# Attention over eight batches: first mixing product over two slots, projections moved, output added by GpSimd, band transposed into the relative products' bank

## The chip, the cores and the metric

The kernel runs on one core of a Trainium2 chip. Five engines work side by side, each through its own list of instructions in order, and meet through semaphores: TensorE (PE; its weight loads are PEld), VectorE (DVE), ScalarE (ACT), GpSimd (POOL) and SyncE (SP), which here only starts DMA transfers. The metric is the device time of one execution in microseconds (us); lower is better.

## What is computed

A block of a network on x of shape 8 x 512 x 128 in float32: attention, mixture of experts, a state-space mixer, the experts again, each behind a layer norm and added to the stream. The change touches attention alone. Cut to what matters:

```python
b, n, _ = x.shape                                  # 8, 512
q, k, v = split(x @ Wqkv.T + bqkv)                 # 16 heads of 64
scores = einsum('bhid,bhjd->bhij', q, k) * SCALE
dist = clip(i - j, -64, 64) + 64
scores = scores + einsum('bhid,ijd->bhij', q, rel_k_emb[dist])
threshold = top_k(scores, 32)[0][..., -1:]         # 32nd largest of each row
attn = softmax(where(scores < threshold, -inf, scores))
v_curr = v
for i in range(3):
    a_v = einsum('bhij,bhjd->bhid', attn, v_curr)
    if i == 0:
        a_v = a_v + einsum('bhij,ijd->bhid', attn, rel_v_emb[dist])
    v_curr = a_v
    res = res + sigmoid(alphas_raw)[i] * v_curr
x = x + merge_heads(res) @ Wout.T + bout
```

## The kernel before

Attention works on one pair of heads of one batch at a time: 8 batches x 8 pairs are 64 iterations (`ITS`). The 512 query rows of an iteration are four tiles T = 0 to 3 of 128 rows, so there are 256 tiles of [128, 2 heads, 512]. All engines run the same order: `run_iterations` calls each engine's `body` once for each *slot*, a pair of iteration i and T, and each body works at that slot on tiles of several ages. `z.back(n)` is the tile that entered n slots ago, `z.iteration(d)` the iteration d away.

For one tile the stages are: at age 0 PE makes the products with the relative keys in banks `RL` and ACT copies them out (`rel`); SP writes them to memory and reads them back skewed (`relj`). At age 2 PE makes the scores in banks `SC`, ACT copies them (`scores`). At age 3 DVE finds the 32 largest of each row: for each head four times `max` (8 values) and three times `match_replace` (L867, L870, L880); POOL then turns the threshold into a mask and adds it (L934 to L949). At age 4 ACT takes exponentials (L794), DVE the reciprocal of the row sums at age 5 (L845, inside `aside`, halfway through the DVE slot) and POOL multiplies (L959). At age 6 PE transposes the probabilities into banks `PT` and ACT copies them to `probs_t`; SP writes a band of them to memory and reads it back skewed (`band`). At age 7 ACT closes the band with sums of what lies left of it, PE transposes it (before: into `PT[0]`) and ACT copies it to `band_t`.

Once an iteration's four tiles are through, three mixing products follow in bank `U`, one of them in each of the slots T = 2, T = 3 and T = 0 of the following iterations. ACT copies each result (`mixed`, L722), PE transposes it, ACT copies it to `u` for the next one, and POOL sums the three with their weights into `res` (L914, L919). At T = 2, three iterations behind, PE multiplies `res` by the output weights in bank `MISC` (L630) and, before the change, DVE adds the result to the stream (L851). The projections to keys (T = 0), values (T = 1) and queries (T = 3) share the bank `MISC` with all this. [...]

`run_iterations` writes iterations -1 to 3 and 62 to 66 out and runs 4 to 61 in a hardware loop of two iterations (8 slots) for each round, on every engine: 29 rounds, 28 jumps back.

Of the kernel before, what the change touches and what calls it, by code (L numbers as in the profile page):

```python
# [16 lines left out]
P = 128  # L17
B, N, D = 8, 512, 128
# [315 lines left out]
class Slots:  # L334


    def __init__(self, g, par, T):
        self.g, self.par, self.i, self.T = g, par, g * 2 + par, T

    def half(self, d):  # L340

        return self.g + (self.par + d) // 2
# [30 lines left out]
def run_iterations(eng, body):  # L373


    first, last = 4, ITS - 2
    for i in range(-1, first):
        for T in range(NT):
            body(Slots(i // 2, i % 2, T), i % 2)
    with eng.Fori(first // 2, last // 2) as g:  # L380
        for par in range(2):
            for T in range(NT):
                body(Slots(g, par, T), par)
    for i in range(last, ITS + 3):
        for T in range(NT):
            body(Slots(i // 2, i % 2, T), i % 2)


def attention(nc, sem, sb, ps, k, t):
# [32 lines left out]
    s.out_made = sem("att_out_made")  # L422
    s.out_added = sem("att_out_added")
    s.bias_added = sem("att_bias_added")
    s.pj_in = [sem(f"att_pj_in{q}") for q in range(2)]
    s.po_in = [sem(f"att_po_in{q}") for q in range(2)]
# [8 lines left out]
    pj = two("pair_j", [P, J_COLS])  # L435
    po = two("pair_o", [P, O_COLS])
    xt = two("xt", [P, N])
# [24 lines left out]

    def mixing(z, par):

        T, old, av = z.T, z.iteration(-3), z.iteration(-2)
        if T == 3 and av is not None:
            return av, 1, par
        if T < 2 and old is not None:
            return old, T + 2, 1 - par
        return None  # L470

    with nc.Block() as block:
        @block.sync
        def _(sp):
            def body(z, par):
                T, q = z.T, z.T % 2
                if T == 2 and (it := z.iteration(1)) is not None:
                    at_pair, at_batch = known(sp, (it % PAIRS) * J_COLS, (it // PAIRS) * N)
                    c0 = known(sp, it - 1)[0]
                    if not early(c0):  # L480
                        sp.wait_ge(s.v_kept, c0)
                    sp.dma_start(pj[1 - par][:, :], t.TJf[:, bass.ds(at_pair, J_COLS)]).then_inc(s.pj_in[1 - par], 16)
                    sp.dma_start(xt[1 - par][:, :], t.XNT[:, bass.ds(at_batch, N)]).then_inc(s.pj_in[1 - par], 16)
                if T == 3 and (it := z.iteration(-1)) is not None:
                    at_out, = known(sp, (it % PAIRS) * O_COLS)
                    c0 = known(sp, it - 1)[0]
                    if not early(c0):
                        sp.wait_ge(s.out_made, c0)
                    sp.dma_start(po[1 - par][:, :], t.TOf[:, bass.ds(at_out, O_COLS)]).then_inc(s.po_in[1 - par], 16)
# [54 lines left out]
        def _(pe):  # L544
# [5 lines left out]
            def body(z, par):  # L550
# [4 lines left out]
                def mix(it, mpar, step):  # L555

                    if not early(it * ORDER + step):
                        pe.wait_ge(s.mixed_kept, it * ORDER + step)
                    for jt in range(NT):
                        for h in range(2):  # L560
                            lhs = v[mpar][:, jt, HEADS[h]] if step == 0 else u[:, jt, h, :]
                            last = nc.tensor.matmul(U[HEADS[h], :], lhs, pt[mpar][:, h, jt, :],  # L562
                                                    start=(jt == 0), stop=(jt == NT - 1 and step > 0))
# [19 lines left out]
                a = z.back(0)  # L583
# [26 lines left out]
                if m and m[1] < 3:  # L610
                    it, step, mpar = m
                    pe.wait_ge(s.mixed_kept, it * ORDER + step)
                    if T == 0 and cur is not None:
                        pe.wait_ge(s.q_kept, cur + 1)
                    if T == 3 and old is not None:
                        pe.wait_ge(s.out_added, old + 1)
                    elif T == 3 and prev is not None:
                        pe.wait_ge(s.v_kept, prev + 1)
                    for jt in range(NT):
# [4 lines left out]
                if T == 2 and old is not None:  # L624
                    pe.wait_ge(s.res_chain, old * 5 + 5)
                    pe.wait_ge(s.po_in[1 - par], 16 * (z.half(-3) + 1))
                    if prev is not None:
                        pe.wait_ge(s.v_kept, prev + 1)
                    for jt in range(NT):
                        last = nc.tensor.matmul(MISC[:, jt * P:(jt + 1) * P], res[:, jt * P:(jt + 1) * P],  # L630
                                                po[1 - par][:, O_W:O_W + P], start=True, stop=True)
                    last.then_inc(s.out_made, 1)

                d = z.back(6)
                if d:
                    it, Td, n = d
                    pe.wait_ge(s.probs, 2 * n + 2)
                    for h in range(2):
                        if h == 0 and not early(n - 1):
                            pe.wait_ge(s.band_kept, n - 1)  # L640
                        elif h == 0 and n > 0:
                            pe.wait_ge(s.probs_kept, 2 * n - 1)
                        if h == 1 and not early(2 * n):
                            pe.wait_ge(s.probs_kept, 2 * n)
# [6 lines left out]
                if T == 0 and cur is not None:  # L651
                    pe.wait_ge(s.pj_in[par], 32 * (z.half(0) + 1))
                    pe.wait_ge(s.q_kept, cur + 1)
                    if m:
                        pe.wait_ge(s.u_kept, m[0] * 2 + 2)
                    nc.tensor.matmul(MISC[:, :], pj[par][:, J_WK:J_WK + P], xt[par][:, :],
                                     start=True, stop=True).then_inc(s.k_made, 1)
                if T == 1 and prev is not None:
# [1272 lines left out]
```

## Time and profile before

| | us |
|---|---|
| median of 3 runs (3132.01 to 3141.05) | 3139.66 |
| the profiled execution, its own time | 3144.04 |
| its span, first to last instruction | 3142.30 |
| attention, from the first `max` of DVE to the end of its last addition to the stream | 64.43 to 2465.46 |

The span is one profiled execution; the profile gives for each engine the busy time, for groups of instructions by line (L867 is line 867) their number, mean duration and what ended the idle time before them, and a timeline. Matmul times are modelled; a releaser is inferred from semaphores, and "issue" stands for time in which an engine waited for nothing that the profile shows. Everything behind 2465 us (experts, mixer, the other norms) is not touched.

### The profile page before, as it was taken

To read this page: it belongs to the slowest core of one execution; us is meant where nothing else is said; L and a number is where in the kernel's file an instruction comes from. 1 tells how busy PE (TensorE), PEld (TensorE's weight loads), DVE (VectorE), ACT (ScalarE), POOL (GpSimd) and SP (SyncE) were. 2 spreads that over 40 slices of the span, in tenths; PEclk is the share of its full clock that TensorE was granted. 3 is DMA by queue.
4 is the path that set the end of the run, shared out by engine and by line. 5 is a ranking of instruction groups with operands and counts; after the bars stand their busy time and mean duration, and the time that the engine had idled before them with its cause. 6 is when DMAs were issued, how large, how long until landed. Compare 5 with 4: busy or idle time off the path is not lost. (4 is left out here: it accounts for less than half of the span.)

```text
span 3142.3 us, 66621 instructions
## 1 busy us (share of the span) xinstructions
PE 2607.6 (83%) x15200; PEld 1498.6 (48%) x15200; DVE 2719.1 (87%) x6639; ACT 2027.7 (65%) x6207; POOL 2163.7 (69%) x2732
## 2 busy tenths in 40 slices
PE   4788888888788888888888888888888685988857
PEld 2444444444444444444444444444444444777743
DVE  5999999999999999999999999999998374765646
ACT  2677777877777777777777777777787152222214
POOL 1788888888888888888888888888888142221105
PEclk7899999999999999999999999999999696776659
DMA  4444444444444444444444444444443000000001
GB/s 119 118 132 134 129 127 125 129 132 125 131 126 129 127 127 127 128 126 130 131 129 126 130 125 134 125 125 131 127 131 100 4 29 14 8 6 1 0 8 48
DMA packets 401017, 318.44 MB, mean 101 GB/s; under 512 B 33246, under 2 KB 388648, under 8 KB 400808
## 3 DMA queue, kind: packets, MB, share of 16 engines
q1 hardware_dynamic: 398660, 314.18, 34.7%
q10 hardware_dynamic: 2148, 2.33, 0.3%
q14 instruction: 182, 1.49, 0.2%
q8 instruction: 27, 0.44, 0.1%
HBM read 139.48 MB, written 136.58 MB: 88 GB/s over the span
## 5 line engine op out<-in xcount | busy, mean ns | idle before, releaser
L870 DVE MAX8 top<-work 128x8 f32<-128x512 f32 x1536 | 980.7, 681 | 0.0
L880 DVE MATCH_REPLACE8 work<-top,work 128x512 f32<-128x512 f32 x1024 | 685.5, 678 | 0.0
L949 POOL TENSOR_TENSOR scores<-scores,cut 128x512 f32<-128x512 f32 x512 | 643.7, 1279 | 0.0
L562 PE MATMUL bank<-probs_t,u 128*64 128x512 f32 x2048 | 467.7, 598 | 1.4 <-ACT u L760 1.4
L794 ACT ACTIVATE probs_of_tile<-scores,minus_max_and_least 128x512 f32<-128x512 f32 x512 | 373.9, 748 | 89.7 <-POOL scores L949 89.2
L959 POOL TENSOR_SCALAR probs_of_tile<-probs_of_tile,inverse 128x512 f32<-128x512 f32 x512 | 349.0, 692 | 84.1 <-DVE inverse L845 61.4
L867 DVE MAX8 top<-scores 128x8 f32<-128x512 f32 x512 | 325.9, 679 | 82.8 <-issue 63.5
L940 POOL TENSOR_SCALAR cut<-scores,minus_max_and_least 128x512 f32<-128x512 f32 x512 | 354.2, 692 | 62.7 <-issue 39.5
L880 DVE MATCH_REPLACE8 work<-top,scores 128x512 f32<-128x512 f32 x512 | 342.7, 678 | 0.0
L771 ACT ACTIVATE probs_t<-bank 128x512 f32<-128x512 f32 x512 | 283.6, 609 | 66.7 <-PE bank L646 66.5
L945 POOL TENSOR_SCALAR cut<-cut 128x512 f32<-128x512 f32 x512 | 305.8, 613 | 21.5
L646 PE MATMUL bank<-identity,probs_of_tile 128*128 128x128 f32 x2048 | 310.9, 302 | 8.5 <-POOL probs_of_tile L959 8.5
L753 ACT ACTIVATE scores<-bank 128x512 f32<-128x512 f32 x512 | 273.5, 584 | 40.6 <-PE bank L605 40.6
L630 PE MATMUL bank<-pair_o,res 128*128 128x128 f32 x512 | 109.5, 382 | 228.7 <-POOL res L919 228.0
L646 PEld LDWEIGHTS bank<-identity,probs_of_tile 128*128 128x128 f32 x2048 | 268.0, 158 | 28.6 <-issue 19.1
L562 PE MATMUL bank<-probs_t,v 128*64 128x512 f32 x1024 | 257.3, 648 | 0.0
L562 PEld LDWEIGHTS bank<-probs_t,u 128*64 128x64 f32 x2048 | 135.7, 136 | 242.2 <-issue 240.4
L934 POOL TENSOR_SCALAR minus_max_and_least<-top 128x4 f32<-128x4 f32 x256 | 50.1, 196 | 238.5 <-issue 194.1
L630 PEld LDWEIGHTS bank<-pair_o,res 128*128 128x128 f32 x512 | 94.3, 276 | 249.4 <-issue 232.3
L731 ACT ACTIVATE band<-band 128x129 f32<-128x129 f32 x512 | 154.3, 303 | 61.6 <-DMA band<-probs_scratch 61.0
L577 PE MATMUL bank<-keys_left,qt 64*128 64x64 f32 (+3 forms) x1024 | 186.1, 441 | 1.8 <-ACT scores L753 1.5
L1634 POOL TENSOR_TENSOR mixer_a_spread<-rest_after,mixer_a 128x1024 f32<-128x1024 f32 x32 | 66.8, 2090 | 174.5 <-PE bank L1491 143.2
(251 smaller groups left out, 5062.7 us busy)
## 6 DMA issues: line engine op xcount, KB each, us to landing
probs_scratch<-probs_of_tile SPq DMA_DIRECT2D x256, 256.0 KB, 2.5
band<-probs_scratch SPq DMA_DIRECT2D x256, 256.0 KB, 3.2
rel_scratch<-rel SPq DMA_DIRECT2D x256, 254.0 KB, 3.1
relj<-rel_scratch SPq DMA_DIRECT2D x256, 128.0 KB, 2.3
relj<-rel_scratch SPq DMA_DIRECT2D x512, 64.0 KB, 2.5
xt<-stream_normed_t SPq DMA_DIRECT2D x64, 256.0 KB, 2.4
pair_j<-table_j SPq DMA_DIRECT2D x64, 193.5 KB, 2.2
pair_o<-table_o SPq DMA_DIRECT2D x64, 66.0 KB, 1.9
```

The costliest lines, as they stand in the source:

```text
L562: last = nc.tensor.matmul(U[HEADS[h], :], lhs, pt[mpar][:, h, jt, :], start=(jt == 0), stop=(jt == NT - 1 and step > 0))
L646: last = nc.tensor.transpose(PT[h][:, jt * P:(jt + 1) * P], t.prob[Td][:, h, HALF + jt * P:HALF + (jt + 1) * P], k.ident[:, :])
L753: nc.scalar.activation(sc[Tb][:, h, :], SC[h][:, :], ACT.Copy).then_inc(s.scores_kept, 1)
L771: nc.scalar.activation(pt[dpar][:, h, :, Td * P:(Td + 1) * P], PT[h][:, :].rearrange("p (j i) -> p j i", j=NT), ACT.Copy).then_inc(s.probs ...
L794: nc.scalar.activation(t.prob[Tx][:, h, HALF:HALF + N], sc[Tx][:, h, :], ACT.Exp, bias=neg[q][:, h, 0:1], accum_out=rs[Tx][:, h:h + 1]).th ...
L867: nc.vector.max(top[q][:, h, 0:8], sc[Tc][:, h, :]).then_inc(s.tops, 1)
L870: nc.vector.max(top[q][:, h, 8 * r:8 * r + 8], work[:, h, :]).then_inc(s.next_tops, 1)
L880: nc.vector.match_replace(out=work[:, h, :], in_to_replace=top[q][:, h, 8 * r:8 * r + 8], in_values=sc[Tc][:, h, :] if r == 0 else work[:, ...
L940: nc.gpsimd.tensor_scalar(cut[:, h, :], sc[Tc][:, h, :], neg[q][:, h, 1:2], STEEP, ALU.add, ALU.mult).then_inc(s.compared, 1)
L945: nc.gpsimd.tensor_scalar(cut[:, h, :], cut[:, h, :], 0.0, NEG, ALU.min, ALU.max).then_inc(s.cut, 1)
L949: nc.gpsimd.tensor_tensor(sc[Tc][:, h, :], sc[Tc][:, h, :], cut[:, h, :], ALU.add).then_inc(s.masked, 1)
L959: nc.gpsimd.tensor_scalar(row, row, inv[Ty][:, h:h + 1], 1.0, ALU.mult, ALU.mult).then_inc(s.probs, 1)
```

## The change

- `run_iterations` has no loop any more: iteration -1, eight batches of eight iterations, and three more iterations are written out. All indices are numbers, so `MISC` products read the tables `table_j`, `table_o` and the normed input where they lie, and the copies to `pair_j`, `xt` and `pair_o` go.
- The first mixing product was made at T = 2, 8 products of 512 columns and 2 for the band. Now columns 0 to 383 are made at T = 1 (with the band for 0 to 255), the rest at T = 2.
- Keys are projected at T = 1, queries at T = 2, both for the next iteration; values at T = 2 after the mixing. ACT copies values at the beginning of T = 3.
- The output product is copied by ACT to `outs` (new), and POOL adds it to the stream; DVE's addition goes.
- The band is transposed into columns 256 to 511 of `RL[0]`, before the probabilities' transposes and not behind them; the next relative product waits until that is copied, and ACT copies it ahead of the exponentials.

```diff
 def run_iterations(eng, body):
-    first, last = 4, ITS - 2
-    for i in range(-1, first):
-        for T in range(NT):
-            body(Slots(i // 2, i % 2, T), i % 2)
-    with eng.Fori(first // 2, last // 2) as g:
-        for par in range(2):
-            for T in range(NT):
-                body(Slots(g, par, T), par)
-    for i in range(last, ITS + 3):
-        for T in range(NT):
-            body(Slots(i // 2, i % 2, T), i % 2)
+    for T in range(NT):
+        body(Slots(-1, PAIRS - 1, T), 1)
+    def batch(g, count=PAIRS):
+        for c in range(count):
+            for T in range(NT):
+                body(Slots(g, c, T), c % 2)
+    for g in range(B):
+        batch(g)
+    batch(B, 3)
...
 # SyncE
-                    sp.dma_start(pj[1 - par][:, :], t.TJf[:, bass.ds(at_pair, J_COLS)]).then_inc(s.pj_in[1 - par], 16)
-                    sp.dma_start(xt[1 - par][:, :], t.XNT[:, bass.ds(at_batch, N)]).then_inc(s.pj_in[1 - par], 16)
...
-                    sp.dma_start(po[1 - par][:, :], t.TOf[:, bass.ds(at_out, O_COLS)]).then_inc(s.po_in[1 - par], 16)
...
 # TensorE
-                a = z.back(0)
+                a, e = z.back(0), z.back(7)
+                if e and not early(e[2]):
+                    pe.wait_ge(s.band_kept, e[2])
...
                 if T == 2 and old is not None:
                     pe.wait_ge(s.res_chain, old * 5 + 5)
-                    pe.wait_ge(s.po_in[1 - par], 16 * (z.half(-3) + 1))
+                    if nxt is not None:
+                        pe.wait_ge(s.k_kept, nxt + 1)
...
+                if e:
+                    pe.wait_ge(s.band_closed, n + 1)
+                    for h in range(2):
+                        last = nc.tensor.transpose(RL[0][:, 2 * P + h * P:2 * P + (h + 1) * P],
+                                                   band[q][:, h, P:2 * P], k.ident[:, :])
+                    last.then_inc(s.band_turned, 1)
...
+                if T == 1 and av is not None:
+                    pe.wait_ge(s.probs_kept, (av * NT + 3) * 2)
+                    pe.wait_ge(s.v_kept, av + 1)
+                    mix(av, par, 0, 0, 3 * P)
+                    pe.wait_ge(s.band_kept, av * NT + 2)
+                    mix_band(0, 2 * P)
+                if T == 2 and av is not None:
+                    pe.wait_ge(s.probs_kept, (av + 1) * NT * 2)
+                    mix(av, par, 0, 3 * P, N)
+                    pe.wait_ge(s.band_kept, (av + 1) * NT)
+                    mix_band(2 * P, N).then_inc(s.mixed, 1)
+                if T == 2 and prev is not None:
+                    if nxt is not None:
+                        pe.wait_ge(s.q_kept, nxt + 1)
...
 # ScalarE
+                if T == 2 and old is not None:
+                    act.wait_ge(s.out_made, old + 1)
...
+                    nc.scalar.activation(outs[:, :], MISC[:, :], ACT.Copy).then_inc(s.out_kept, 1)
...
 # VectorE
-                    if old is not None and T == 2:
-                        dve.wait_ge(s.out_made, old + 1)
...
-                        Xb = k.X[:, bass.ds((old // PAIRS) * N, N)]
-                        nc.vector.tensor_tensor(Xb, MISC[:, :], Xb, ALU.add).then_inc(s.out_added, 1)
...
 # GpSimd
+                if z.T == 2 and (old := z.iteration(-3)) is not None:
+                    pool.wait_ge(s.out_kept, old + 1)
...
+                    Xb = k.X[:, tokens(old)]
+                    nc.gpsimd.tensor_tensor(Xb, outs[:, :], Xb, ALU.add).then_inc(s.out_added, 1)
```

The end of DVE's loop body before, over the jump back (L380), with the last tile of a round; register instructions (L369, L844) stand between the operations:

```order
L867 MAX top<-scores 128x8
L880 MATCH_REPLACE work<-top,scores 128x512 x2
...
L870 MAX top<-work 128x8
L369 REGISTER_ALU
L870 MAX top<-work 128x8
L380 REGISTER_ALU
L380 COMPARE_AND_BRANCH
```

A tile of DVE now; the next one follows it in the list:

```order
L866 MAX top<-scores 128x8 x2
L879 MATCH_REPLACE work<-top,scores 128x512 x2
L869 MAX top<-work 128x8 x2
L879 MATCH_REPLACE work<-top,work 128x512 x2
L850 RECIPROCAL inverse<-row_sums 128x2
L869 MAX top<-work 128x8 x2
L879 MATCH_REPLACE work<-top,work 128x512 x2
L869 MAX top<-work 128x8 x2
```

The jump, the register instructions and the addition L851 are no longer in DVE's list.

PE's slot T = 2 in the loop before (`bank` is any bank; `probs_t,v` is the first mixing product):

```order
L605 MATMUL bank<-relj,identity 64x192 x4
L625 ISA
L626 REGISTER_ALU
L630 MATMUL bank<-pair_o,res 128x128 x4
...
L646 MATMUL bank<-identity,probs_of_tile 128x128 x8
L678 REGISTER_ALU
L680 ISA
L684 MATMUL bank<-identity,band 128x128 x2
...
L562 MATMUL bank<-probs_t,v 64x512 x8
L693 MATMUL bank<-band_t,rel_values 64x512 x2
```

The end of slot T = 1 and slot T = 2 now:

```order
L665 MATMUL bank<-stream_normed_t,table_j 128x512
L554 MATMUL bank<-probs_t,v 64x384 x8
L561 MATMUL bank<-band_t,rel_values 64x256 x2
...
L632 MATMUL bank<-table_o,res 128x128 x4
L641 MATMUL bank<-identity,band 128x128 x2
L653 MATMUL bank<-identity,probs_of_tile 128x128 x8
L673 MATMUL bank<-stream_normed_t,table_j 128x512
L554 MATMUL bank<-probs_t,v 64x128 x8
L561 MATMUL bank<-band_t,rel_values 64x256 x2
L693 MATMUL bank<-table_j,stream_normed_t 128x128 x4
```

Three quarters of the mixing stand in T = 1, the two projections for queries and values in T = 2, and the band ahead of the probabilities.

## Rows read from the trace of the kernel before

**Rows 1.** Windows: straight code, loop, straight code; busy (count) of PE, PEld, DVE, ACT, POOL, clock
```profile
100.00:178.00 78.00, 63.44 (x368) 32.84 (x369) 78.00 (x189) 58.35 (x183) 64.55 (x87) 0.87 0.43 123
178.00:2325.00 2147.00, 1859.75 (x11633) 995.73 (x11629) 2075.07 (x4938) 1650.37 (x5176) 1797.65 (x2383) 0.94 0.45 128
2325.00:2420.00 95.00, 77.85 (x494) 42.79 (x492) 95.00 (x228) 72.75 (x226) 83.84 (x110) 0.95 0.40 114
```

**Rows 2.** The view of line L867, DVE's first max of a tile: idle before (us, times)
```profile
  issue: 63.5, 25
```

**Rows 3.** Timeline of DVE in the loop: start, us, engine, line, operation
```profile
1046.50 1.26 DVE L867 MAX8 top<-scores 128x8 f32<-128x512 f32 x2
...
1051.58 0.67 DVE L851 TENSOR_TENSOR stream<-bank,stream 128x512 f32 x1
...
1055.87 1.27 DVE L867 MAX8 top<-scores 128x8 f32<-128x512 f32 x2
...
1067.52 1.29 DVE L867 MAX8 top<-scores 128x8 f32<-128x512 f32 x2 [2.79 <-ACT scores L753]
```

**Rows 4.** Timeline of DVE, the last tiles, in straight code
```profile
2385.31 1.27 DVE L867 MAX8 top<-scores 128x8 f32<-128x512 f32 x2
...
2411.62 1.27 DVE L867 MAX8 top<-scores 128x8 f32<-128x512 f32 x2
```

**Rows 5.** Timeline of POOL, the first instruction for each tile, slots T = 3 to T = 2
```profile
1029.19 0.20 POOL L934 TENSOR_SCALAR minus_max_and_least<-top 128x4 f32<-128x4 f32 x1 [1.06 <-issue]
...
1046.02 1.27 POOL L919 TENSOR_TENSOR res<-res,tmp 128x512 f32<-128x512 f32 x1
1047.26 0.19 POOL L934 TENSOR_SCALAR minus_max_and_least<-top 128x4 f32<-128x4 f32 x1
...
1056.10 0.20 POOL L934 TENSOR_SCALAR minus_max_and_least<-top 128x4 f32<-128x4 f32 x1 [1.79 <-issue]
```

**Rows 6.** Timeline of PE, one iteration between two jumps
```profile
1020.04 0.60 PE L577 MATMUL bank<-keys_left,qt 64*128 64x192 f32 x4
...
1047.53 1.13 PE L630 MATMUL bank<-pair_o,res 128*128 128x128 f32 x8 [3.15 <-POOL res L919]
1048.49 1.04 PE L646 MATMUL bank<-identity,probs_of_tile 128*128 128x128 f32 x8
1050.30 0.44 PE L684 MATMUL bank<-identity,band 128*128 128x128 f32 x2 [0.77 <-ACT probs_t L771]
1050.66 3.65 PE L562 MATMUL bank<-probs_t,v 128*64 128x512 f32 x16
...
1055.11 0.59 PE L577 MATMUL bank<-keys_left,qt 64*128 64x192 f32 x4
```

**Rows 7.** Timeline of ACT, slots T = 1 and T = 2
```profile
1042.15 0.67 ACT L782 ACTIVATE rel<-bank 128x254 f32<-128x254 f32 x2
...
1046.68 0.31 ACT L731 ACTIVATE band<-band 128x129 f32<-128x129 f32 x1 [1.27 <-DMA band<-probs_scratch]
...
1048.70 1.06 ACT L753 ACTIVATE scores<-bank 128x512 f32<-128x512 f32 x2
...
1050.61 0.67 ACT L782 ACTIVATE rel<-bank 128x254 f32<-128x254 f32 x2
```

**Rows 8.** The view of the tile `band` in the loop: waits for its DMA, time to landing
```profile
  DMA band<-probs_scratch: 54.2, 48
...
DMA to landing us min/median/max: 2.8/3.2/4.0
```

**Rows 9.** Timeline of PE and DVE at attention's start and in its straight code
```profile
51.41 2.08 PE L671 MATMUL bank<-xt,pair_j 128*128 128x512 f32 x2 [4.02 <-DMA xt<-stream_normed_t]
...
64.43 1.29 DVE L867 MAX8 top<-scores 128x8 f32<-128x512 f32 x2 [10.90 <-ACT scores L753]
...
107.33 1.22 PE L592 MATMUL bank<-rel_keys,qt 64*128 64x254 f32 x4 [3.44 <-issue]
```

**Rows 10.** Timeline of DVE at attention's end
```profile
2464.77 0.69 DVE L851 TENSOR_TENSOR stream<-bank,stream 128x512 f32<-128x512 f32 x1 [23.80 <-PE bank L630]
```

More of the change, by code:

```diff
@@ L433, in two @@
         return [sb(f"{name}{q}", shape) for q in range(2)]
-    pj = two("pair_j", [P, J_COLS])
-    po = two("pair_o", [P, O_COLS])
-    xt = two("xt", [P, N])
+    outs = sb("outs", [P, N])
     qt = two("qt", [P, N])
@@ L553, in body, with mix @@
                 cur, nxt = z.iteration(0), z.iteration(1)
-                def mix(it, mpar, step):
-                    if not early(it * ORDER + step):
+                def mix(it, mpar, step, lo=0, hi=N):
+                    if lo == 0 and not early(it * ORDER + step):
                         pe.wait_ge(s.mixed_kept, it * ORDER + step)
@@ L638, in body @@
                     for h in range(2):
[L639 to L644, printed above, removed]
+                        if not early(2 * n + h - 1):
+                            pe.wait_ge(s.probs_kept, 2 * n + h - 1)
                         for jt in range(NT):
@@ new lines, in body @@
+                if T == 2 and nxt is not None:
+                    if old is not None:
+                        pe.wait_ge(s.out_kept, old + 1)
+                    else:
+                        pe.wait_ge(s.k_kept, nxt + 1)
+                    nc.tensor.matmul(MISC[:, :], t.TJ[:, z.pair(1), J_WQ:J_WQ + P], k.XNT[:, tokens(nxt)],
+                                     start=True, stop=True).then_inc(s.q_made, 1)
+                if T == 1 and av is not None:
+                    pe.wait_ge(s.probs_kept, (av * NT + 3) * 2)
+                    pe.wait_ge(s.v_kept, av + 1)
+                    mix(av, par, 0, 0, 3 * P)
+                    pe.wait_ge(s.band_kept, av * NT + 2)
+                    mix_band(0, 2 * P)
@@ L674, in body @@
-                e = z.back(7)
-                if e:
-                    it, Te, n = e
-                    q = Te % 2
-                    pe.wait_ge(s.band_closed, n + 1)
-                    if d:
-                        pe.wait_ge(s.probs_kept, 2 * (n + 1) + 1)
-                    elif not early(n):
-                        pe.wait_ge(s.band_kept, n)
-                    for h in range(2):
-                        last = nc.tensor.transpose(PT[0][:, h * P:(h + 1) * P], band[q][:, h, P:2 * P], k.ident[:, :])
-                    last.then_inc(s.band_turned, 1)
@@ L687, in body @@
-                if T == 2 and av is not None:
-                    pe.wait_ge(s.probs_kept, (av + 1) * 2 * NT)
-                    pe.wait_ge(s.v_kept, av + 1)
-                    mix(av, par, 0)
-                    pe.wait_ge(s.band_kept, (av + 1) * NT)
-                    for h in range(2):
-                        last = nc.tensor.matmul(U[HEADS[h], :], t.relv[:, :], bt[par][:, h, :],
-                                                start=False, stop=True)
-                    last.then_inc(s.mixed, 1)
```

155 lines of the change are left out of this document (74 added, 81 removed).

## The prediction

> **What bounds the kernel now.** I read the windows first [rows 1]. In attention DVE is busy 2075 of the loop's 2147 us and for the whole of the two stretches of straight code around it; PE has 87%, POOL 84%, ACT 77%. So inside attention DVE sets the time, if nobody makes it wait. It does stop: the view of its first `max` of a tile has 25 waits with no releaser, 63.5 us, 2.54 each [rows 2]. The timeline shows what they are [rows 3]. Tile starts at 1046.50 and 1055.87 lie 9.37 apart, with the addition to the stream (L851) between; the next at 1067.52 is 11.65 later, with 2.79 of idle. In the straight code behind the loop three tiles take 26.31, that is 8.77 each [rows 4]. So a tile costs DVE 8.77 us, an addition 9.37 - 8.77 = 0.60 more, and the slot over the loop's jump back some 2.7 more. This row puts the 2.79 down to ACT's score copy, but such gaps come once in eight tiles, 28 times, and 25 of them have no releaser; and ACT's copies of the scores end well ahead, at 1049.76 for the tile that DVE begins at 1055.87, 6.1 later [rows 3, 7]. The gaps are the jump's. Since DVE's list is its own, these three terms must add up: from the first `max` at 64.43 to that of the last tile at 2411.62 are 2347.19 us for 255 tiles [rows 4, 9]. 255 x 8.77 = 2236.4. One addition an iteration falls into 61 of these slots, 61 x 0.60 = 36.6. The rest, 74.2 us, over 28 jumps is 2.65 each, which agrees with the 2.54.
>
> **What goes from the bound.** (1) The jumps: 28 x 2.65 = 74.2 us. The changed DVE list has one tile behind the other, as in the straight stretches of before, where DVE is busy for 78.00 of 78.00 and 95.00 of 95.00 us [rows 1]. The Trainium skill, page "Runtime: NRT & Kernel Launch", section "Instruction fetch mechanics", says that a taken branch to a target outside the two buffered blocks waits for a fetch, while straight code is fetched ahead with the cost mostly hidden; by that rule, too, the gaps go and none comes in their place, and the trace agrees where it has straight code. (2) The additions: 61 inside, and one more for the last tile, 62 x 0.60 = 37.2. Together 111.4 us, 3.5%.
>
> **What the others pay, and whether it stays covered.** After the change DVE asks for an iteration each 4 x 8.77 = 35.08 us; before it was 2347.19 / 63.75 = 36.8. Every other engine must do one in less.
>
> POOL: in an iteration without a jump, 4 x 8.77 + 0.60 = 35.68 long, it stands idle before two of four tiles, 1.06 and 1.79 [rows 5], and works through between the others. Its work is 35.68 - 2.85 = 32.8, the short gaps between instructions among it. The new addition is a two-input operation on 128 x 512, as L919: 1.27 [rows 5]. Makes 34.1, 1.0 under DVE's. It stands where POOL waited 1.79, behind T = 1's tile, so it is hidden: 0 us. POOL is the closest to becoming the bound by its own work. The Trainium skill, "GPSIMD Engine Reference", section "Engine selection", advises against this step: elementwise additions belong on VectorE, GpSimd being about twice as slow for two inputs. The rows agree on the price (1.27 against 0.67), but it is paid on the engine with room. By its factor the change would lose 0.6 us an iteration if both engines were equally full; they are not.
>
> PE: from 1020.04 to 1055.11 an iteration, of which it waited 3.15 and 0.77 [rows 6], so about 31.1 of work at the higher clock. New is only that the mixing is cut in two. A quarter of 3.65 is 0.91; if the 16 passes of 128 columns cost no less than the transposes' passes (1.04 for 8) they take 2.08, so the cut costs 0 to 1.2 us. Work 31 to 32.3 of 35.08. The four slots become even, about 8 each, where T = 1 was short and T = 2 long. PE's added waits: behind `band_closed` stand now the probabilities' transposes; at T = 2 the values wait for the query copy, which ACT makes behind the exponentials. I follow that one, as PE's next scores queue behind it. The exponentials wait for POOL's mask, which follows DVE by some 6 us; copy 0.7, value product 1.0, then 2.1 to the next scores, 1.1 for ACT's copy after the band sums: some 12.5 us behind the end of a DVE tile, and DVE needs them two tiles, 17.5, behind it. 5 us of room; 0 us.
>
> ACT: busy 77%, 28.4 us an iteration; the copy `outs` adds 0.6. Fine by sum, but there is a ring: ACT's `rel` copy ends, SP issues the store and then the load of the band, that lands, ACT makes the band sums, scores, probabilities and `rel` again. In T = 1 to 2 it took from 1042.82 to 1051.28, 8.46, with ACT waiting on the DMA in between [rows 7]. The copy `outs` stands inside it: 8.46 + 0.47 (spacing of the other copies of this size) = 8.93, over 8.77. But only for one slot in four; the others have no `outs`, and in the loop ACT waited on this DMA in 48 of 233 slots [rows 8]. I take a whole iteration at 8.93 + 3 x 8.46 = 34.3 and 0 us, with an upper end of 4 x 8.93 = 35.7, which would be 0.6 x 64 = 40 us.
>
> Transfers: 192 copies of SP (`pair_j`, `xt`, `pair_o`) go from its queue. They were hidden and go at 0 us; the queue they leave also carries the band, so their going speaks for the ring, if anything. At the start PE waited 4.02 for `xt` [rows 9]; without it keys come first (2.1 and ACT's two copies), so queries start at about 52.0 where they started at 51.41: +0.6. At the end, behind DVE's last tile, nothing hides: 23.80 of the last wait is the chain of three mixings for the last iteration [rows 10]. Three quarters of the first one now start before the band is closed, -2.5; the last output goes through ACT (0.6 and a semaphore) and POOL (1.27) and not DVE (0.69), +1.3. Sum -1.2. Between -4 and +3 for both ends together.
>
> **The sum**, against the profiled execution's own 3144.04 (span 3142.30 and 1.74 around it): - 74.2 - 37.2 + 0.6 - 1.2 = 3032. The median of the runs lies 4.4 below that execution, so as a median **3028**.
>
> **Rivals.** (A) DVE stays the bound in every slot: 3028, with 3018 to 3040 for the ends, the clock and the untouched rest. (B) A ring or an engine becomes the bound, at 35.3 to 36.0 an iteration: the ACT and DMA ring at 4 x 8.93, or POOL at 34.1 with its start delayed. For it: a slot at 8.93 and POOL at 97%. Against: both sums are under 35.08, and short delays are taken up by 5 us of room. Price 0.2 to 0.9 x 64 = 13 to 58 us: 3041 to 3086. (C) The jumps' 2.65 are not the jump but the fetch of so many instructions, and the written out list pays it again once in eight to ten tiles: only the additions go, 3028 + 74 = 3102. For it: the gap follows a count of instructions as well as a jump. Against: no gap in 173 us of straight code [rows 1], some 20 tiles. (D) Slower. PE has about ten times DVE's instructions, and its straight code shows one stall of 3.44 us with no releaser, at 107.33 [rows 9]. If written out code brings two such stalls an iteration, PE needs 31.1 + 6.9 = 38.0 against 36.8 before: 3140 + 1.2 x 64 = 3217. It decides from (36.8 - 31.1) / 2 = 2.85 us a stall. Against: one is in the trace, in some ten iterations of straight code, not two in each.
>
> **Chances.** A 0.72, B 0.16, C 0.05, D 0.04, and 0.03 for something between A and less. What a measurement of this kernel can tell from no change is about 0.3%, 9 us; A, B and C are all faster by more. Faster 0.94, same 0.02, slower 0.04. The range takes in A whole and B's lower two thirds: 3014 to 3068.
>
> **What would show it.** Right: tile starts of DVE 8.77 apart throughout, idle before its first `max` 11 us in all, first to last 2236 us; POOL busy about 94% in attention and waiting some 0.5 before T = 2's tile; PE waiting less than 1 before the output product. B: DVE idle before the first `max` with ACT's scores as releaser, spread over many tiles. C: idle marked issue at even distances. D: PE's idle marked issue, growing. Wrong altogether if a tile itself takes DVE longer than 8.77, as when POOL's new addition disturbs it; the rows show it at the same 8.77 whatever POOL does.

## The result

| | before | changed |
|---|---|---|
| median | 3136.55 us (3132.01 to 3141.05, 4 runs) | 3024.56 us (3008.46 to 3027.00, 4 runs) |
| ratio | | 0.963, 95% interval 0.960 to 0.967 |
| the profiled execution, its own time | 3144.04 | 3027.00 |
| its span | 3142.30 | 3025.3 |
| first `max` of DVE's first tile to first `max` of its last tile | 2347.19 | 2235.90 |

The changed kernel is 3.7% faster, 112 us. Of these, 111.3 lie between DVE's first and last tile. The forecast was 3028, and 2236 for that stretch. It started from a median of 3139.66 for the kernel before; the median of all four runs is 3136.55, and this makes up 3.1 of the 3.4 us by which the changed kernel's median lies under the forecast. Below, "the tile stretch" is always this last row: 255 tiles, taken from the starts of the first `max` of each tile in the timeline.

The view of DVE's first `max` of a tile, now L866 (before it had "issue: 63.5, 25" [rows 2]). Columns: line, engine, operation, count; duration in ns, least, median, most; first and last start (the last is the second head's, 0.6 behind the first head's); then what DVE waited for, us and times:

```profile
L866 DVE MAX8 top<-scores x512: 662/665/753, 65.8 to 2302.3; 128x8 f32<-128x512 f32 x171
its engine sat idle before it (us, times) until:
  ACT scores L759: 10.8, 1
```

The one wait is that before the first tile. From there on DVE never stops. The timeline of DVE around 1020 us says the same tile by tile: 8.77 apart, where before the same stretch had 9.37 and 11.65 [rows 3].

```profile
1021.48 1.26 DVE L866 MAX8 top<-scores 128x8 f32<-128x512 f32 x2
...
1030.25 1.26 DVE L866 MAX8 top<-scores 128x8 f32<-128x512 f32 x2
```

The window over nearly all of attention, in the columns of [rows 1]:

```profile
178.00:2285.00 2107.00, 1863.34 (x13208) 1025.75 (x13204) 2107.00 (x5045) 1744.80 (x5404) 1936.59 (x2524) 0.99 0.43 121
```

DVE is busy for 2107.00 of 2107.00 us. POOL is at 1936.59 / 2107 = 92%, PE at 88%, ACT at 83%. PE's granted clock was 0.99 of full speed (2.4 GHz), where it had been 0.94.

PE over slots T = 1 and T = 2 of one iteration, against [rows 6] (start, duration, line, what, idle before and releaser):

```profile
1034.60 2.80 PE L554 MATMUL bank<-probs_t,v 128*64 128x384 f32 x16
...
1039.90 1.16 PE L632 MATMUL bank<-table_o,res 128*128 128x128 f32 x8
1041.08 0.44 PE L641 MATMUL bank<-identity,band 128*128 128x128 f32 x2
...
1043.59 1.09 PE L554 MATMUL bank<-probs_t,v 128*64 128x128 f32 x16
1044.51 0.60 PE L561 MATMUL bank<-band_t,rel_values 128*64 128x256 f32 x4
1046.87 1.16 PE L693 MATMUL bank<-table_j,stream_normed_t 128*128 128x128 f32 x8 [1.76 <-ACT qt L830]
1047.96 0.59 PE L576 MATMUL bank<-keys_left,qt 64*128 64x192 f32 x4
...
1049.45 0.66 PE L606 MATMUL bank<-relj,identity 64*64 64x256 f32 x8
```

The 3.15 us before the output product are gone. In their place PE waits 1.76 before the value product for the query copy. Nothing shows of it on DVE, though the slot is longer than a DVE tile: from one slot's band transposes at 1041.08 to the next slot's at 1050.54 are 9.46 us. POOL in the same iteration, at the places of [rows 5]:

```profile
1021.70 0.20 POOL L940 TENSOR_SCALAR minus_max_and_least<-top 128x4 f32<-128x4 f32 x1 [0.94 <-issue]
...
1046.83 1.27 POOL L925 TENSOR_TENSOR stream<-outs,stream 128x512 f32<-128x512 f32 x1
...
1056.78 0.20 POOL L940 TENSOR_SCALAR minus_max_and_least<-top 128x4 f32<-128x4 f32 x1 [0.97 <-issue]
```

The new addition takes the 1.27 that its neighbour took, and POOL is left with one pause of about 1 us an iteration.

### The profile page after: what moved, and what is told of

It is laid out like the page before. It is cut to its first block and busy times, and to the rows that moved or that the text cites. A ratio compares the mean times of both kernels' runs of the same rounds, so it can differ in the third digit from the quotient of the medians.

```text
span 3025.3 us, 61812 instructions
## 1 busy us (share of the span) xinstructions
PE 2549.6 (84%) x16480; PEld 1500.3 (50%) x16480; DVE 2678.7 (89%) x6575; ACT 2070.2 (68%) x6271; POOL 2245.4 (74%) x2796
## 5 line engine op out<-in xcount | busy, mean ns | idle before, releaser
L866 DVE MAX8 top<-scores 128x8 f32<-128x512 f32 x512 | 327.5, 686 | 10.8 <-ACT scores L759 10.8
L653 PE MATMUL bank<-identity,probs_of_tile 128*128 128x128 f32 x2048 | 276.1, 280 | 6.0 <-POOL probs_of_tile L965 6.0
L554 PE MATMUL bank<-probs_t,v 128*64 128x384 f32 (+1 forms) x2048 | 252.6, 389 | 0.0
L641 PE MATMUL bank<-identity,band 128*128 128x128 f32 x512 | 109.2, 295 | 165.9 <-ACT band L746 164.8
L653 PEld LDWEIGHTS bank<-identity,probs_of_tile 128*128 128x128 f32 x2048 | 240.6, 145 | 6.4 <-POOL probs_of_tile L965 6.4
L554 PEld LDWEIGHTS bank<-probs_t,v 128*64 128x64 f32 x2048 | 124.0, 138 | 171.8 <-ACT probs_t L783 99.1
L796 ACT ACTIVATE rel<-bank 128x254 f32<-128x254 f32 x512 | 174.1, 412 | 2.8 <-PE bank L593 2.8
```

Source lines behind the costliest of these rows:

```text
L554: last = nc.tensor.matmul(U[HEADS[h], lo:hi], lhs, pt[mpar][:, h, jt, lo:hi], start=(jt == 0 and lo == 0), stop=(jt == NT - 1 and step > 0))
L653: last = nc.tensor.transpose(PT[h][:, jt * P:(jt + 1) * P], t.prob[Td][:, h, HALF + jt * P:HALF + (jt + 1) * P], k.ident[:, :])
L866: nc.vector.max(top[q][:, h, 0:8], sc[Tc][:, h, :]).then_inc(s.tops, 1)
```

## The experiments

The forecast had put a price on the jumps and on DVE's addition, and nothing on the three other moves (mixing split, projections moved, band moved). So the first question was whether those moves matter at all, and the later ones followed from the answer. "DVE stretch" is the tile stretch of the profiled execution; the changed kernel's is 2235.90. Each time stands with its ratio to the kernel before from the same chip, since that one moved by a few us between chips (medians 3131.24 to 3139.11).

### 1. The code written out, nothing else (e1_unroll)

```diff
-    with eng.Fori(first // 2, last // 2) as g:
-        for par in range(2):
-            for T in range(NT):
-                body(Slots(g, par, T), par)
+    for i in range(-1, ITS + 3):
+        for T in range(NT):
+            body(Slots(i // 2, i % 2, T), i % 2)
```

> The kernel before with its loop written out and nothing else changed: same order of work, copies of the tables by SyncE, addition to the stream by VectorE. Theory (the 28 gaps belong to the jumps): tile starts 8.77 us apart, 9.37 where an addition lies between, no gap; the time falls by 28 x 2.65 = 74 us, a ratio of 0.976 to the kernel before. Rival (the gaps come with the fetch of so many instructions): no gain, ratio 1.000. Rival (the old order can't keep up without the pauses of the jumps): VectorE waits for ScalarE's scores in many tiles, a ratio between 0.98 and 1.

Measured: 3106.13 us, ratio 0.989 (0.985 to 0.993); DVE stretch 2320.82. Of the 74 us only 26 arrive on DVE and some 30 in the time (29 between the medians, 35 by the ratio), as in the second rival of the expectation. The view of DVE's first `max` shows what came instead of the jumps:

```profile
L859 DVE MAX8 top<-scores x512: 662/676/698, 66.1 to 2387.6; 128x8 f32<-128x512 f32 x171
...
  ACT scores L745: 39.8, 40
```

The jumps' idle is gone, and DVE now waits for ACT's scores, 40 times. The old order can't do an iteration in 35.68 us (four tiles and an addition): it takes 2320.82 / 63.75 = 36.4. The 36.8 of the kernel before hid that.

### 2. Written out, and GpSimd adds the output; the rest in the old order (e2_unroll_pooladd)

On top of experiment 1 ACT's `outs` and POOL's addition of the change, at the same slot.

> As e1_unroll, and the output product copied by ScalarE and added to the stream by GpSimd, still in the old order: first mixing product whole at T = 2, projections at T = 0, 1, 3, band transposed behind the probabilities in their bank. Theory (moving the mixing, the projections and the band takes nothing from VectorE's list and is worth nothing): every tile 8.77 us, ratio 0.964, the same as the full change within 0.2%. Rival (the even order is what lets TensorE and ScalarE keep up at 35.08 us an iteration): VectorE waits for scores, ratio 0.97 or more.

Measured: 3159.60 us, ratio 1.009 (1.006 to 1.011), so 0.9% slower than the kernel before; DVE stretch 2366.55. Both terms of the sum are in this kernel, and both are lost.

```profile
L858 DVE MAX8 top<-scores x512: 666/676/697, 66.1 to 2433.3; 128x8 f32<-128x512 f32 x171
...
  ACT scores L747: 122.4, 80
```

The timelines of one T = 2 slot show the chain, ACT, PE and DVE in turn:

```profile
1022.27 0.31 ACT L725 ACTIVATE band<-band 128x129 f32<-128x129 f32 x1 [1.98 <-DMA band<-probs_scratch]
...
1025.72 1.09 ACT L771 ACTIVATE probs_t<-bank 128x512 f32<-128x512 f32 x2
...
1033.07 0.69 ACT L716 ACTIVATE mixed<-bank,pair_o 128x512 f32<-128x512 f32 x1 [4.03 <-PE bank L687]
...
1035.17 1.09 ACT L747 ACTIVATE scores<-bank 128x512 f32<-128x512 f32 x2 [0.51 <-PE bank L599]
```

```profile
1026.48 0.41 PE L678 MATMUL bank<-identity,band 128*128 128x128 f32 x2 [4.04 <-ACT probs_t L771]
1026.81 5.35 PE L556 MATMUL bank<-probs_t,v 128*64 128x512 f32 x16
...
1032.95 0.59 PE L571 MATMUL bank<-keys_left,qt 64*128 64x192 f32 x4
```

```profile
1035.90 1.29 DVE L858 MAX8 top<-scores 128x8 f32<-128x512 f32 x2 [2.01 <-ACT scores L747]
```

Read it forward. ACT waits for the band's DMA, makes the sums, the scores' copy, `outs` and then the copies of the transposed probabilities. PE waits for the last of these, because the band goes into the same bank. Behind it stands the whole first mixing, and behind that the next tile's score products. PE had stood 4.04 us, and the mixing takes 5.35 instead of the 3.65 of [rows 6]; the window over it shows a granted clock of 0.67 of full speed, the one over the wait before it 1.00 (columns as in [rows 1]):

```profile
1021.00:1026.40 5.40, 1.44 (x14) 1.20 (x12) 5.40 (x14) 4.10 (x15) 2.96 (x4) 1.00 0.64 194
1026.80:1032.00 5.20, 5.20 (x18) 1.61 (x19) 5.20 (x15) 2.24 (x8) 4.87 (x8) 0.67 0.42 117
```

So part of the mixing ran at the lower level, 1.2 GHz. This is not one slot's accident: the page of the profile has 336.6 us for the 64 mixings of this run, 5.26 each, against 257.3 and 4.02 in the kernel before. ACT stands 4.03 us for its result, and the band's next round over DRAM, which ACT has to pass on, starts that much later. Two things in this picture are changed by the change: where the band stands (theory B), and how long the block ahead of the scores is (theory M). Experiments 4 to 7 part them. The lower clock is a third thing, which no run sets by itself: 64 times 5.26 - 3.65 are 103 of the 131 us that this kernel's stretch is longer than the changed kernel's.

### 3. The changed kernel with DVE's addition back (e3_after_dveadd)

DVE adds from the bank, ACT's `outs` and POOL's addition go; the rest is the changed kernel.

> The changed kernel with the addition to the stream back on VectorE, straight from the bank, and no copy by ScalarE. Theory (an addition costs VectorE 0.60 us and nobody else matters): 37 us more than the changed kernel, ratio 0.976 to the kernel before; tiles at 8.77 and one in four at 9.37. Rival (GpSimd's addition costs something back that this kernel regains): less than 30 us more.

Measured: 3063.13 us, ratio 0.976 (0.973 to 0.979); DVE stretch 2274.19, 38.3 more. Two kinds of tile are left, and one in four carries the addition. The timeline of DVE:

```profile
1017.92 1.26 DVE L866 MAX8 top<-scores 128x8 f32<-128x512 f32 x2
...
1023.00 0.66 DVE L850 TENSOR_TENSOR stream<-bank,stream 128x512 f32<-128x512 f32 x1
...
1027.29 1.26 DVE L866 MAX8 top<-scores 128x8 f32<-128x512 f32 x2
```

The first two starts lie 9.37 apart; the next tile, without an addition, begins 8.77 later at 1036.06. The addition's 0.60 was priced rightly (61 x 0.60 = 36.6; two of these tiles took 0.8 and 0.9 longer still).

### 4. The band in its new place, all else as in experiment 2 (f1_band)

```diff
+                if e:
...
+                        last = nc.tensor.transpose(RL[0][:, 2 * P + h * P:2 * P + (h + 1) * P],
+                                                   band[q][:, h, P:2 * P], k.ident[:, :])
...
-                        last = nc.tensor.transpose(PT[0][:, h * P:(h + 1) * P], band[q][:, h, P:2 * P], k.ident[:, :])
```

> The code written out with GpSimd's addition and the old order of the rest (e2_unroll_pooladd, 3159.6 us), with one thing taken from the change: the band transposed into the relative products' bank, ahead of the exponentials' transposes, and copied by ScalarE ahead of its exponentials. Theory B (the band's place sets the ring of 37.4 us per iteration: the transposes waited behind the transposed exponentials' copy 70 times, up to 4.9 us, and the next mixing behind them): first to last maximum about 2245 to 2270 us, time about 3030 to 3060. Theory M (the first mixing as one block of 3.65 to 5.4 us ahead of the scores is what makes VectorE wait): VectorE still waits 1 to 2 us once an iteration, time 3120 or above.

Measured: 3083.73 us, ratio 0.983 (0.979 to 0.987); DVE stretch 2278.54. Better than experiment 2 by 88 us of the stretch, and still 43 above the changed kernel's. The figure falls between the two theories' ranges. The mixing takes 4.59 on average here (293.6 us for 64), 60 us in all over 3.65 each, so a lower clock alone could account for the 43.

### 5. The changed kernel with the first mixing whole (f2_whole)

```diff
-                if T == 1 and av is not None:
...
-                    mix(av, par, 0, 0, 3 * P)
-                    pe.wait_ge(s.band_kept, av * NT + 2)
-                    mix_band(0, 2 * P)
...
-                    mix(av, par, 0, 3 * P, N)
+                    mix(av, par, 0)
```

> The changed kernel with one thing undone: the first mixing is issued as one block of 512 columns in one step again, instead of over two. Theory B (the band's place is what matters): 3025 to 3040 us, VectorE's tiles still at 8.77. Theory M (the split matters): one wait of 1 to 2 us of VectorE per iteration, 64 of them, so 3090 to 3150.

Measured: 3169.21 us, ratio 1.012 (1.007 to 1.016); DVE stretch 2372.53. With this alone undone the change loses everything and 1% on top. The price, 136.6 us of stretch or 2.1 an iteration, is more than either theory's waits would make.

```profile
L861 DVE MAX8 top<-scores x512: 662/676/698, 64.4 to 2437.6; 128x8 f32<-128x512 f32 x171
...
  ACT scores L754: 138.5, 74
```

PE in its T = 2 slot, then DVE:

```profile
1028.32 0.52 PE L641 MATMUL bank<-identity,band 128*128 128x128 f32 x2 [1.92 <-ACT band L741]
1028.63 1.91 PE L653 MATMUL bank<-identity,probs_of_tile 128*128 128x128 f32 x8
1030.34 1.84 PE L673 MATMUL bank<-stream_normed_t,table_j 128*128 128x512 f32 x2
1032.10 3.65 PE L554 MATMUL bank<-probs_t,v 128*64 128x512 f32 x16
1035.59 1.03 PE L561 MATMUL bank<-band_t,rel_values 128*64 128x512 f32 x4
1036.55 1.16 PE L688 MATMUL bank<-table_j,stream_normed_t 128*128 128x128 f32 x8
...
1039.13 0.66 PE L606 MATMUL bank<-relj,identity 64*64 64x256 f32 x8
...
1040.21 0.38 PE L641 MATMUL bank<-identity,band 128*128 128x128 f32 x2
```

```profile
1040.58 1.29 DVE L861 MAX8 top<-scores 128x8 f32<-128x512 f32 x2 [2.14 <-ACT scores L754]
```

From the band's transposes at 1028.32, which start when ACT has closed the band, to the next tile's last score product at 1039.13 are 10.8 us. In the changed kernel the two lines lie at 1041.08 and 1049.45, so 8.4, with 1.76 of waiting in it. The whole slot, from its band transposes to those of the next slot at 1040.21, takes 11.9 us, and PE doesn't wait in it. That is 3.1 over 8.77, and the question is what the other three slots can give back. They begin at 1040.21, 1048.36 and 1056.90, and the next iteration's long slot at 1065.55, so they take 8.15, 8.54 and 8.65. In each of them PE has time to spare, and waits for ACT's band sums (0.55, 1.33 and 2.02), while ACT waits for the band's DMA. Their mean of 8.45 is the pace of the ring from band sums to scores, round through the DRAM, to the next band sums, for which the forecast had 8.46. Together they give back 1.0. The four slots make 37.2 us, and that is this kernel's pace: 2372.53 / 63.75 = 37.2.

A part of the 11.9 is the clock. Behind PE's wait of 1.92 the probabilities' transposes took 1.91 and the query product 1.84, where the changed kernel's took 1.04 and 1.13, and the granted clock from 1028.3 to 1032.1 was 0.55. Over all such slots of the run it was 0.88 on average, at a mean length of 11.8. At the higher level this slot would be 1.6 shorter, 10.3, and the iteration 35.6: an estimate that leaves 0.6 of the 2.1 us to the length of the block and gives the rest to the clock. No run here holds the clock still, so this division is not shown. What is shown is that cutting the block takes away both.

### 6. The changed kernel with the band in its old place (f3_bandold)

The edit is that of experiment 4 turned round, in the changed kernel, with ACT's copy behind the exponentials again.

> The changed kernel with another thing undone: the band is transposed into the probabilities' bank, behind the exponentials' transposes and the projections, and its copy on ScalarE stands behind the exponentials. Theory B: the band sums reach the DMA later, the ring grows past 35.08 us per iteration, 3050 to 3150 us. Theory M: no change, 3020 to 3030.

Measured: 3023.90 us, ratio 0.964 (0.961 to 0.967); DVE stretch 2235.84. Nothing changed; DVE's waits before its first `max` are one, at the start:

```profile
  ACT scores L765: 9.9, 1
```

Theory B falls as the account of the changed kernel: the band's place gives 88 us where the mixing is whole and nothing where it is split.

### 7. Experiment 2 with the split alone (g1_split)

The projections, the band and the fetches of `pair_j`, `xt`, `pair_o` stay old; the mixing is that of the change, 384 columns at T = 1 and 128 at T = 2.

> e2_unroll_pooladd (written out, GpSimd adds, everything else in the old order: 3159.6 us) with the split first mixing alone: 384 columns a step earlier, 128 in the old step. Undoing the split in the changed kernel cost 145 us, undoing the band's move nothing. If the split alone is what lets the order hold 8.77 us per tile: about 3025 to 3035, no waits of VectorE. If the projections' new place is needed as well: 3060 to 3110, with waits of VectorE once an iteration.

Measured: 3019.56 us, ratio 0.963 (0.960 to 0.966); DVE stretch 2235.97. The view of DVE's first `max`, and PE at T = 2:

```profile
  ACT scores L756: 10.7, 1
```

```profile
1041.60 0.41 PE L685 MATMUL bank<-identity,band 128*128 128x128 f32 x2 [0.79 <-ACT probs_t L780]
1041.93 1.09 PE L556 MATMUL bank<-probs_t,v 128*64 128x128 f32 x16
1045.45 0.65 PE L563 MATMUL bank<-band_t,rel_values 128*64 128x256 f32 x4 [2.42 <-ACT band_t L813]
1046.03 0.90 PE L578 MATMUL bank<-keys_left,qt 64*128 64x192 f32 x4
```

The same time as the changed kernel (the intervals lie over one another). From the band's transposes to the next scores' start 4.4 us, with 2.42 of waiting among them, where experiment 2 had 6.5, 5.35 of them for the mixing. Of the three moves (mixing, band, projections) the split is the one that the change needs; the projections' new place and the band's are worth nothing beside it.

### 8. The same with the loop kept (h1_loop_split)

> The same as g1_split, with the loop of two iterations kept (28 jumps back). The prediction priced a jump at 2.65 us of VectorE, 74.2 in all: if nothing else hides or adds to it, this is g1_split + 74, so about 3100 if that one is at 3025. If the prefetch gap is taken up by a slack that the new order has, it is under g1_split + 40; if the jumps of the other engines add their own waits, over g1_split + 90.

Measured: 3117.46 us, ratio 0.995 (0.992 to 0.997); DVE stretch 2325.21, 89.2 above experiment 7. All other tiles are at 8.77; the 28 over the jump are at 11.0 to 12.6. The view of the first `max`, and one jump in the timeline:

```profile
L875 DVE MAX8 top<-scores x512: 662/677/700, 64.2 to 2390.0; 128x8 f32<-128x512 f32 x171
...
  issue: 75.8, 24
  ACT scores L764: 21.3, 5
```

```profile
1056.33 1.29 DVE L875 MAX8 top<-scores 128x8 f32<-128x512 f32 x2 [3.15 <-issue]
```

A jump costs DVE 89.2 / 28 = 3.19 us here, more than the 2.65 of the kernel before. In the time the jumps are some 100 us by the two ratios; in the profiled executions 10 us beyond the stretch lie behind the last tile's start, a part that is nearly all untouched code and that differs by as much between other executions (720 us here, 710 in experiment 7, 724 in the changed kernel). The expectation of 74 was low by the dearer jump; why that is dearer wasn't tested.

### 9. How much room POOL and the ring have (e4_after_pool1, after_pool2, act_in, act_out)

One and two more `tensor_tensor` of 128x512 on POOL in each iteration of the changed kernel:

> The changed kernel with one more two-input operation of 128x512 on GpSimd in each iteration, on data that nobody waits for. Theory (GpSimd's work is 34.1 us of 35.08, so it has 0.9 us of room): 1.28 - 0.9 = 0.3 to 0.4 us an iteration, 19 to 26 us more than the changed kernel, and VectorE waits somewhere in each iteration. Rival (the bound is soft, GpSimd's lag never reaches VectorE): 0 us. Rival (GpSimd is already part of the bound): 1.28 x 64 = 82 us more.

> The changed kernel with two more 128x512 operations of 1.28 us on GpSimd per iteration (one gave +12.6 us, from a room of 1.08 us). If GpSimd's room is really used up by the first, the second costs its whole length: 64 x 1.28 = 82 us more, 3119 us, tile sum 2326. If something else gave the 12.6 us (a semaphore hop, a later query copy), it costs about 13 more again: 3050.

Measured: 3037.19 us, ratio 0.969 (0.966 to 0.972), DVE stretch 2243.72; and 3111.17 us, ratio 0.992 (0.989 to 0.995), DVE stretch 2320.96. The first operation costs 7.8 us of stretch (12.6 in the time), the second 77.2, which is 1.21 for each of 64, nearly its whole 1.28. The first is under the 19 to 26 us expected, the second near its 82. So POOL's room is 2 x 1.28 - 85.1 / 64 = 1.2 us an iteration.

An extra 128x512 copy of ACT in each tile, once inside the ring and once behind the exponentials, where ACT waits for the band anyway:

```diff
                         nc.scalar.activation(sc[Tb][:, h, :], SC[h][:, :], ACT.Copy).then_inc(s.scores_kept, 1)
+                    nc.scalar.activation(spare[T][:, :], k.XNT[:, 0:N], ACT.Copy)
```

> The changed kernel with one extra 128x512 copy of ScalarE (0.6 us) in every tile, right behind the scores' copy, so ahead of the transposes' copies, the exponentials and the band's round over DRAM. The prediction's rival B: the ring over ScalarE and the DMA takes 34.3 us of the 35.08, so room 0.8 us per iteration, 4 copies put 2.4 us in: ring 36.7, +1.6 x 64 = about +100 us, 3125. If that ring has more room than worked out (f3_bandold, with the band's copy behind the exponentials, lost nothing): 3025 to 3045.

> The changed kernel with the same extra 128x512 copy of ScalarE per tile as act_in, but behind the exponentials, where ScalarE waits for the band's DMA anyway (190 us of waiting in all in the changed kernel, 183 times). If act_in's +78 us came from a ring (band sums, scores' copy, transposes' copies, exponentials, DMA, band sums), this costs nothing or little: 3025 to 3040. If it came from ScalarE's load as such (1745 us busy of 2107, plus 4 x 0.6 us per iteration), it costs the same 78 us: about 3100.

Measured: 3102.42 us, ratio 0.989 (0.986 to 0.992), DVE stretch 2315.15; and 3038.15 us, ratio 0.969 (0.966 to 0.973), DVE stretch 2247.29. The waits of DVE for the first kernel, then for the second:

```profile
  ACT scores L760: 64.0, 140
```

```profile
  ACT scores L760: 18.5, 15
```

The same work costs 79 us of stretch in one place and 11 in the other, so it is the ring and not ACT's load. In the ring ACT spaces the copy 0.52 from its neighbour: 4 x 0.52 = 2.1 us more an iteration, of which 79.25 / 64 = 1.24 come through. If each copy makes the ring longer by its whole 0.52, the ring has 0.85 us of room and takes about 34.2 of the 35.08; that is an estimate.

### All together

DVE stretch in us, all with GpSimd's addition and all but the last row written out:

| first mixing | band | projections | DVE stretch | experiment |
|---|---|---|---|---|
| whole | old | old | 2366.55 | 2 |
| whole | new | old | 2278.54 | 4 |
| whole | new | new | 2372.53 | 5 |
| split | old | old | 2235.97 | 7 |
| split | old | new | 2235.84 | 6 |
| split | new | new | 2235.90 | the changed kernel |
| split | old | old, loop kept | 2325.21 | 8 |

The three rows at 2236 are DVE's own 255 x 8.77. Where the mixing is whole, the projections moved beside it cost another 94 us, because T = 2 then holds the query product, the whole mixing and the value product in one slot: from one slot's band transposes to the next slot's it takes 9.9 us in experiment 4 (1018.11 to 1028.01) and 11.9 in experiment 5. (Two combinations with the band or the projections moved alone were not run. Rows with the projections new also have no fetches for them.)

## Why the prediction was right, and what it left out

**The bound and its unit.** DVE sets the time at 8.77 us a tile: right. The changed kernel's 2235.90 stands against 2236.4.

**The jumps, -74.2.** Right as a term of this change. The 74.2 was what is left of the stretch once tiles and additions are taken off, so that the three terms add up is no test of it. The tests are the trace of before, in which 28 tiles take 11.0 to 12.2 us, 61 take 9.4 and all the others 8.77, and the runs without the loop, in which no such gap is left. Experiment 8 shows that the 28 jumps are worth 89.2 in the order of the changed kernel; since both jumps and additions go altogether, only what the kernel before paid counts.

**The additions, -37.2.** Right: experiment 3 puts 38.3 back.

**The covers.** POOL: 1.0 us of room forecast, 1.2 measured (experiment 9). It was busy 92% of the time, 94 expected, and its pause lies before T = 3's tile, 0.94, and not the 0.5 before T = 2's. The ACT and DMA ring: 34.3 forecast, about 34.2 estimated from the extra copy, though only as a mean. ACT waited for the band's DMA in 182 slots, in 48 in the loop before [rows 8], which on its own looked like rival B; but none of these waits reaches DVE, whose one idle stretch is that before the first tile. The value product behind the query copy: PE waited 75.6 us in 58 slots for it, 2.3 at most, within the 5 us of room. PE before the output product: 0.9 us in all. The rows, first ACT's and then PE's:

```profile
ACT band L737 <- DMA band<-probs_scratch: 188.9, 182, 2.8
...
PE bank L693 <- ACT qt L830: 75.6, 58, 2.3
```

**The ends, +0.6 and -1.2.** Against the bias addition, the last thing ahead of attention, DVE's first `max` came 0.1 earlier, not 0.6 later. From the last tile's start to the end of attention 53.84 became 51.58, -2.3, where -1.2 and the last addition's 0.6 had been set. The untouched rest took 672.0 instead of 676.8; these 4.8 are most of why the profiled execution came out at 3027.0 and not at 3032. That part is spread, not effect.

**Rivals.** C (the gaps are the fetch of so many instructions) falls: there is no gap in 2236 us of straight code. The Trainium skill, "Runtime: NRT & Kernel Launch", section "Instruction fetch mechanics", calls the stall at a taken branch a reason for full unrolling, and the traces agree, with 3.15 us of idle over a jump in experiment 8 and none without. D (PE stalled by its fetch) is not seen either: no wait of PE is left that DVE feels. Its premise was misread: the windows count 11633 matmuls against 4938 instructions of DVE [rows 1], 2.4 times as many, or 4.7 with the weight loads, and not about ten. Rival B (a ring or an engine becomes the bound; not the theory B of the experiments) didn't happen in the changed kernel, but it is what happens in it once the split is undone, by the slot T = 2, of which the forecast only said that it was long before the change and would be even with the others after it.

**What the prediction left out.** It took each engine's sum of work in an iteration, 31 to 32.3 us for PE and 34.3 for the ring, and let all that is below 35.08 pass. By that test experiments 2 and 5 should have run at DVE's pace as well: their sums are the same, and experiment 5 does less work by the cut. PE was in fact busy for only 86% and 85% of their time (1774.48 and 1767.91 of 2072 us), some 32 us an iteration. They lose 131 and 137 us. So the mixing's split, priced there only as 0 to 1.2 us of extra work for PE, is what lets the other two terms arrive: without it the sum of 111 us would have come out at plus 25. The forecast came out because the change carried that split; the sum had not shown that it was needed, and to that extent its success was luck. What the sum lacked is the ring's pace as a floor in each slot: with 11.9 in one slot and 8.46 in the other three, an iteration takes 37.3. It also took the mixing at 3.65 throughout, where it took 5.26 on average in experiment 2 behind PE's longer waits. The row that could have told it stood in the trace of before: PE's 3.65 of mixing between the band's transposes at 1050.30 and the next scores at 1055.11 [rows 6]; ACT waited for the result in all 64 iterations, 168.7 us together. And the -74.2 had no such check: with the loop alone taken out, the same sum would have given 3061 where 3106 was measured.

## What to carry to other kernels

A stall on the bounding engine may hide a ring that is barely shorter. Before such a stall is priced as gained, work out the pace of the other chains slot by slot. For each slot take the longer of two times, the engine's own work in it and the ring that passes through it, and only then add up the iteration: a long slot is harmless as long as the others can give its excess back (9.46 in the changed kernel), and they can't give back more than the ring leaves them (11.9 in experiment 5). A long block of products that stands ahead of what the bound waits for is worth cutting even where the cut costs work, the more so as it may run at the lower clock behind a wait. And moves that only help together must be tested together: here the band's move looks worth 88 us or nothing, depending on the split.

## What the runs showed of the hardware

- A jump back in a loop of eight tiles a round cost DVE 2.65 us in the kernel before and 3.19 us in experiment 8, for the same loop without its two additions. What sets the difference is open.
- The same 16 passes of 512 columns took 3.65 us in one place and 5.35 in another, where PE had stood for 4.04 us before, at a granted clock of 0.67 over the stretch. On average over the 64 blocks of a run they took 4.02 us in the kernel before, 5.26 in experiment 2, 4.59 in experiment 4 and 3.93 in experiment 5 (matmul times are modelled). So a wait of PE can cost more than its own length when a long block follows at once.
- POOL at 95% busy (1961.06 of 2072 us in the run with one more operation) left DVE's tile at 8.77 us in 240 of 255 cases: POOL's work on 128x512 tiles didn't slow DVE's.
